# The end of a normalisation wave: one batch's output rows on VectorE, two batches normalised on ScalarE and GpSimd, low product parts issued last

## The reference, cut to what matters

```python
x = _layernorm(x + _L0_attn_ref(...))
x = _layernorm(x + _L0_ffn_ref(...))     # h = _layer_norm(h + interf, ln4_g[1], ln4_b[1]) is its last step
x = _layernorm(x + _L1_attn_ref(...))    # q, k = elu(x W) + 1; v = x W; kv = k^T v; z = 1 / (q . sum k); out = (q kv) z Wo
x = _layernorm(x + _L1_ffn_ref(...))     # six blocks of gelu(x W1 + b1) W2 + b2 + x
```

## Time and profile before

| what | value |
|---|---|
| median of 3 runs | 1039.43 us |
| lowest of them | 1037.92 us |
| the profiled execution's own time | 1038.4 us |
| its span, first to last instruction | 1036.7 us |
| mean granted TensorE clock over the span | 0.986 of full speed |
| TensorE busy | 986.6 us (95% of the span) |
| VectorE, ScalarE, GpSimd busy | 735.5, 606.8, 370.9 us |

### The profile page before, as it was taken

The page is one execution under the profiler, slowest core; times in us unless marked ns, Lnnn a source line. Parts: engine busy times, 40 slices in busy tenths (PEclk is TensorE's granted clock), DMA queues, the critical chain, the costliest instruction groups (busy, mean ns, idle before and its releaser), DMA issues.

```text
span 1036.7 us, 18193 instructions
## 1 busy us (share of the span) xinstructions
PE 986.6 (95%) x6627; PEld 824.5 (80%) x6627; DVE 735.5 (71%) x2003; ACT 606.8 (59%) x1177; POOL 370.9 (36%) x646
## 2 busy tenths in 40 slices
PE   6999999999999898889999999999999999999997
PEld 5555655555758797778899999999999999999997
DVE  5666787867647779867557768766776877677764
ACT  5566667655259774456546666554666655456660
POOL 4444374552131474443722222322222232222600
PEclk9899999998999999999999999999999999999999
DMA  7000000013020001022201010110101011010101
GB/s 254 23 2 21 3 22 22 23 43 102 22 87 4 1 2 41 1 102 62 82 1 42 1 41 1 42 41 2 41 1 42 1 41 42 1 42 1 41 23 60
DMA packets 29234, 36.91 MB, mean 36 GB/s; under 512 B 1780, under 2 KB 26584, under 8 KB 29144
## 3 DMA queue, kind: packets, MB, share of 16 engines
q1 hardware_dynamic: 24728, 31.15, 9.4%
q10 hardware_dynamic: 4416, 4.59, 1.4%
HBM read 31.40 MB, written 4.20 MB: 34 GB/s over the span
## 4 chain that ended last, share of the span: by engine, by line
PE 56%; DVE 4%; POOL 2%; issue 1%; ACT 1%; DVEq 0%; POOLq 0%; ACTq 0%
PE ps L1930 25%; PE ps L1947 24%; PE ps L1820 2%; PE ps L1902 2%; DVE ln_stats L2337 1%; PE ps L1960 1%; PE ps L1871 1%; POOL hs L1717 1%; POOL x_b L1717 0%; PE ps L1834 0%; DVE amp L2373 0%; PE ps L1849 0%; PE ps L1862 0%; PE ps L1771 0%; DVE att L2429 0%
## 5 line engine op out<-in xcount | busy, mean ns | idle before, releaser
L2173 ACT ACTIVATE G<-ps,bias_col 128x512 f32<-128x512 f32 x192 | 135.8, 707 | 176.5 <-PE ps L1930 167.9
L1947 PE MATMUL ps<-w_h,G_h 128*128 128x256 f32 x736 | 204.3, 278 | 0.0
L1947 PE MATMUL ps<-w_l,G_h 128*128 128x256 f32 x736 | 204.0, 277 | 0.0
L1947 PE MATMUL ps<-w_h,G_l 128*128 128x256 f32 x736 | 204.0, 277 | 0.0
L2477 DVE TENSOR_TENSOR G_l<-G,G_h 128x512 fp32r<-128x512 f32 x192 | 155.8, 819 | 59.7 <-ACT G_h L2174 59.7
L1747 POOL TENSOR_TENSOR x_a<-xn,mlp_g 128x1024 f32<-128x1024 f32 x20 | 68.0, 3401 | 333.8 <-DVE xn L2505 333.8
L708 ACT ACTIVATE probs<-ps 128x512 f32<-128x512 f32 (+3 forms) x256 | 98.3, 441 | 98.0 <-PE ps L848 97.2
L1930 PE MATMUL ps<-xT_h,w_h 128*128 128x512 f32 x384 | 151.7, 395 | 0.3 <-issue 0.3
L1930 PE MATMUL ps<-xT_h,w_l 128*128 128x512 f32 x384 | 149.9, 390 | 0.0
L1930 PE MATMUL ps<-xT_l,w_h 128*128 128x512 f32 x384 | 149.5, 389 | 0.0
L1119 DVE CUSTOM_DVE_ANT_0 ps<-ps,q_mask 128x128 f32<-128x128 f32 (+3 forms) x256 | 120.7, 512 | 29.9 <-PE ps L837 29.4
(11 more groups left out here) (320 smaller groups left out, 2094.5 us busy)
## 6 DMA issues: line engine op xcount, KB each, us to landing
w_raw<-L_ffn_W_T SPq DMA_DIRECT2D x12, 1024.0 KB, 5.1
hs<-L_attn_hidden_states SPq DMA_DIRECT2D x8, 512.0 KB, 3.9
x_kept<-hs SPq DMA_DIRECT2D x4, 512.0 KB, 3.2
w_raw<-x_kept SPq DMA_DIRECT2D x2, 1024.0 KB, 5.3
out<-xn SPq DMA_DIRECT2D x3, 512.0 KB, 3.0
w_raw<-L_ffn_ent_w_T SPq DMA_DIRECT2D x1, 1024.0 KB, 10.2
w_raw<-L_ffn_ent_pw SPq DMA_DIRECT2D x1, 1024.0 KB, 12.3
heads_T<-neg_rows SPq DMA_DIRECT2D x64, 2.0 KB
```

Source lines behind the costliest of these rows:

```text
L1947: mm = pe.matmul(ps[:, 4 + t // 2, (t % 2) * D:(t % 2 + 1) * D], x[b % 2][f][:, t * P:(t + 1) * P], w2_chunk(w, f), start=(k == 0), stop=( ...
L2173: act.activation(G32[n % 4], bank, ACT.Gelu, bias=bias)
```

## The change

Batch 0's output rows are made on VectorE (`output_rows`) and no longer on GpSimd. VectorE makes the low parts of batch 3's last turn ahead of `moments_sum(0)`, and `output_low(0)` ahead of `sum_up(1)`. For batches 2 and 3 `centre` and `sum_up` are gone: VectorE makes an offset (-mean x root, `offset_last`), ScalarE normalises from PSUM (`normalise_last`), GpSimd multiplies by the row last_g, and VectorE adds the residual (`add_residual`), later in its list than `sum_up` was; `moments_sum(2)` and `root("sum", 2)` are later in theirs too. The first unit of a batch waits for the high parts only, and issues its two products with low parts last; the first three units take the banks in the order 2, 0, 1.

```diff
-    ON_SCALAR = [key for b in range(B) for key in (("stage", END, b), ("sum", b))] + [("next", 0), ("next", 1)]
+    ON_SCALAR = [("stage", END, 0), ("sum", 0), ("stage", END, 1), ("sum", 1), ("stage", END, 2), ("stage", END, 3),
+                 ("sum", 2), ("sum", 3), ("next", 0), ("next", 1)]
...
+    def unit_bank(n):
+
+        return (n - 1) % 3 if n < 3 else n % 3
...
# GpSimd
-        for b in range(B):
+        whole(("sum", 1), g.x_b[:, RT:2 * RT, :], sums(1))
+        pool.wait_ge(rows_in, 16)
+        for b in (2, 3):
+            pool.wait_ge(wave["a_last"], b - 1)
+            pool.tensor_tensor(normed(b), normed(b), bcast(last_g, 1, [P, RT, D]), ALU.mult).then_inc(wave["g_gain"], 1)
+        for b in (2, 3):
             whole(("sum", b), g.x_b[:, b * RT:(b + 1) * RT, :], sums(b))
...
# TensorE, unit
             if at == 0:
-                pe.wait_ge(wave["v_tl"], wave_done(b))
-            if n == 2:
+                pe.wait_ge(wave["a_th"], wave_done(b))
+            if n == 0:
 
                 centred(pe, 1)
-            if n >= 3:
-                pe.wait_ge(second["a_exp"], n - 2)
-                pe.wait_ge(second["a_v"], values(n - 3))
...
+            if n >= RT - 1:
+                before = n - 2 if n < 5 else n - 3
+                pe.wait_ge(second["a_exp"], before + 1)
+                pe.wait_ge(second["a_v"], values(before))
...
+            if at == 0:
+                products = [products[k] for k in (0, 1, 3, 4, 2, 5)]
+            for i, (lhsT, rhs) in enumerate(products):
+                if at == 0 and i == 4:
+                    pe.wait_ge(wave["v_tl"], wave_done(b))
+                mm = pe.matmul(ps[:, unit_bank(n), :], lhsT, rhs, start=(i == 0), stop=(i == 5))
...
# ScalarE
+        def normalise_last(b):
+            root = rooted(act, "stage", END, b)[1]
+            act.wait_ge(wave["v_offset"], b - 1)
+            for k in range(RT):
+                ins = act.activation(normed(b)[:, k, :], banks(b)[k], ACT.Identity,
+                                     bias=offsets[:, b - 2, k:k + 1], scale=root[:, k:k + 1])
+            ins.then_inc(wave["a_last"], 1)
...
         unit(0, 2)
+        normalise_last(2)
         unit(0, 3)
+        root("stage", END, 3)
         unit(0, 4)
-        root("sum", 2)
         for c in range(KC):
             output_high(1, c)
         unit(0, 5)
+        normalise_last(3)
         unit(1, 0)
-        root("stage", END, 3)
         unit(1, 1)
         unit(1, 2)
+        root("sum", 2)
         unit(1, 3)
...
# VectorE
+        def offset_last(b):
+
+            moments, root = rooted(v, "stage", END, b)
+            v.scalar_tensor_tensor(offsets[:, b - 2, :], moments[:, :, 0], -1.0, root, ALU.mult, ALU.mult
+                                   ).then_inc(wave["v_offset"], 1)
+
+        def add_residual(b):
+
+            v.wait_ge(wave["g_gain"], b - 1)
+            chain.step(v.tensor_tensor(amp[:, b, :, :].rearrange("p c s -> p (c s)"),
+                                       normed(b).rearrange("p t d -> p (t d)"),
+                                       g.x_a[:, b * RT:(b + 1) * RT, :].rearrange("p t d -> p (t d)"), ALU.add))
+
+        def output_rows():
+
+            moments, root = rooted(v, "sum", 0)
+            for k in range(RT):
+                ins = v.tensor_scalar(g.x_b[:, k, :], sums(0)[:, k, :], moments[:, k, 0:1], root[:, k:k + 1],
+                                      ALU.subtract, ALU.mult)
+            ins.then_inc(wave["v_whole"], 1)
...
                 if (st, b) == (END - 1, B - 2):
                     centre(0)
                     sum_up(0)
+                elif (st, b) == (END - 1, B - 1):
                     run(moments_sum(0))
-                elif (st, b) == (END - 1, B - 1):
-                    run(moments(END, 1))
+                    steps = moments(END, 1)
+                    run(steps, 1)
+                    output_rows()
+                    run(steps)
...
         centre(1)
-        sum_up(1)
         for c in range(KC):
             output_low(0, c)
+        sum_up(1)
         run(moments_sum(1))
         unit(0, 0)
         run(moments(END, 2))
         unit(0, 1)
-        centre(2)
+        offset_last(2)
         unit(0, 2)
-        sum_up(2)
+        run(moments(END, 3))
         unit(0, 3)
-        run(moments_sum(2))
         unit(0, 4)
+        offset_last(3)
         for c in range(KC):
             output_low(1, c)
         unit(0, 5)
         block_diagonal(0)
-        run(moments(END, 3))
         unit(1, 0)
         divide(0, 0)
-        centre(3)
         unit(1, 1)
         divide(0, 1)
-        sum_up(3)
+        add_residual(2)
+        run(moments_sum(2))
         unit(1, 2)
         unit(1, 3)
         attention_low(0)
+        add_residual(3)
         run(moments_sum(3))
         unit(1, 4)
```

More of the change, by code:

```diff
@@ L246, in build @@
         g.wave = sems(top, nc, "a_trig v_turns v_h a_hh v_gated g_zero v_c p_lin v_mv g_scale g_chain a_norm p_T a_th v_tl a_l1 v_l1 v_chain "
-                      "v_scale v_mean a_root v_center g_eps", "wave_")
+                      "v_scale v_mean a_root v_center v_whole v_offset a_last g_gain g_eps", "wave_")
         g.second = sems(top, nc, "blocks_in b2_in g_ones p_unit a_exp a_v v_unit p_kv v_bd p_num v_att v_z p_attT a_atth v_attl "
@@ L1500, in rest @@
     eps = put(nc, "root_eps", g.small, ROOT + 14 * RT, [1])
+    offsets = put(nc, "root_offsets", g.small, ROOT + 16 * RT, [2, RT])
     TILE = NORM + 14 * RT
@@ L1542, in rest @@
     ON_VECTOR = [("stage", 0, 0)]
-    ON_SCALAR = [key for b in range(B) for key in (("stage", END, b), ("sum", b))] + [("next", 0), ("next", 1)]
-    WHOLE = [*(("sum", b) for b in range(B)), *(("next", b) for b in range(B))]
+    ON_SCALAR = [("stage", END, 0), ("sum", 0), ("stage", END, 1), ("sum", 1), ("stage", END, 2), ("stage", END, 3),
+                 ("sum", 2), ("sum", 3), ("next", 0), ("next", 1)]
+    WHOLE = [*(("sum", b) for b in range(1, B)), *(("next", b) for b in range(B))]
     ON_GPSIMD = [key for key in NORMS + WHOLE if key not in ON_VECTOR + ON_SCALAR]
@@ L1552, in normalised @@
     def normalised(eng, *key):
-        if key in WHOLE:
+        if key == ("sum", 0):
+            eng.wait_ge(wave["v_whole"], 1)
+        elif key in WHOLE:
             eng.wait_ge(second["g_whole"], WHOLE.index(key) + 1)
@@ L1559, in centred @@
     def centred(eng, b):
-        eng.wait_ge(wave["v_center"], b + 1)
+        if b < 2:
+            eng.wait_ge(wave["v_center"], b + 1)
+        else:
+            eng.wait_ge(wave["a_last"], b - 1)
     def rooted(eng, *key):
@@ L1801, in unit @@
             if at == 0:
-                pe.wait_ge(wave["v_tl"], wave_done(b))
-            if n == 2:
+                pe.wait_ge(wave["a_th"], wave_done(b))
+            if n == 0:
                 centred(pe, 1)
-            if n >= 3:
-                pe.wait_ge(second["a_exp"], n - 2)
-                pe.wait_ge(second["a_v"], values(n - 3))
-            i = 0
+            if n >= RT - 1:
+                before = n - 2 if n < 5 else n - 3
+                pe.wait_ge(second["a_exp"], before + 1)
+                pe.wait_ge(second["a_v"], values(before))
+            products = []
             for c in range(KC):
@@ L1818, in unit @@
                              (g.xT_l[:, b, c, cols], g.wkv_h[:, c, :]))
-                for lhsT, rhs in parts:
-                    mm = pe.matmul(ps[:, n % 3, :], lhsT, rhs, start=(i == 0), stop=(i == 5))
-                    i += 1
+                products += parts
+            if at == 0:
[4 more added lines that the diff above has]
+                mm = pe.matmul(ps[:, unit_bank(n), :], lhsT, rhs, start=(i == 0), stop=(i == 5))
             mm.then_inc(second["p_unit"], 1)
@@ L2106, in unit @@
                 act.wait_ge(second["v_unit"], n - 1)
-            act.activation(ex[:, n % 2, 0:width], ps[:, n % 3, 0:width], ACT.Exp)
-            act.activation(pos[:, n % 2, 0:width], ps[:, n % 3, 0:width], ACT.Relu).then_inc(second["a_exp"], 1)
+            act.activation(ex[:, n % 2, 0:width], ps[:, unit_bank(n), 0:width], ACT.Exp)
+            act.activation(pos[:, n % 2, 0:width], ps[:, unit_bank(n), 0:width], ACT.Relu).then_inc(second["a_exp"], 1)
             if j >= KC:
@@ L2114, in unit @@
                 act.activation(v1[:, b % 2, j - KC, :, 0:P],
-                               ps[:, n % 3, D:2 * D].rearrange("p (m n) -> p m n", m=KC),
+                               ps[:, unit_bank(n), D:2 * D].rearrange("p (m n) -> p m n", m=KC),
                                ACT.Copy).then_inc(second["a_v"], 1)
@@ L2338, in statistics @@
             chain.step(ins)
+            yield
             chain.settle()
```

## The result

The changed kernel takes 1043.48 us (median of 5 runs, 1043.2 to 1047.13) against 1039.1 us for the kernel before in the same comparison. The ratio is 1.0047, with a 95% interval of [1.0032, 1.0061]: about 4.4 us slower. One of the five runs of the kernel before took 2357.16 us; the ratio goes without it. The forecast was 1041.2 us with a range up to 1043.2, so the median lies 0.3 us outside. The profiled execution takes 1043.2 us, its span 1041.5 us, against 1038.4 and 1036.7.

What follows compares the result with a forecast made beforehand. TensorE, busy all its time from 497 us, was taken to bound the kernel by how late it gets there. A net delay of +1.8 us and +1.0 for the clock on 1038.4 gave 1041.2 us, range 1037.8 to 1043.2.

Steps and rivals of the forecast that it cites:

- The 9.0 us margin: Before the change, batch 2's rows lay ready at 423.93, 9.0 us before TensorE transposed them at 432.94.
- The lead ahead of it: Before final_turn(2, 0), TensorE was to run earlier: 1.8 us at final_turn(0), 0.3 at final_turn(1), 1.7 on reaching final_turn(2, 0).
- the walk had x_b end last: At final_turn(1): GpSimd's rows of batch 1 start at 410.6, take 5.75 us and end at 416.4, 0.3 us earlier.
- Rival (4): Before 423.7: ScalarE's eight added ACTIVATEs hold up its units, no lead arises, add_residual(2) is 1.7 us later; 1042.9 us, chance 0.08.
- Rival (3): TensorE's later waits at 440 to 470 us swallow the delay, clock holds: 1038.4 us, down to 1036.7; chance 0.14.
- Rival (1): Same stall at final_turn(2, 0) but no fall of TensorE's clock: +1.8, 1040.2 us, chance 0.2.
- Rival (2): GpSimd and VectorE exclude each other fully, x_b takes 6.1, clock stretch falls on work: +2.4 + 1.7, 1042.5 us, chance 0.08.
- GpSimd's multiply by last_g is done long before ... has 5 us to spare: Batch 2's multiply, ahead of add_residual(2), starts at 416.4, takes 4.03 us at worst and has 5 us to spare.
- that rule on x_b beside add_residual alone: At batch 2's rows: by the exclusion rule x_b would wait 1.21 us for the add, 6.1 instead of 5.5.
- the forecast had 11.70 us: From numerators(0, 1) at 423.7, through divide, residual, statistics, root and x_b (5.5 us), to final_turn(2, 0) at 435.4.
- The clock was taken at 1.0: Behind the 4.2 us stall TensorE's clock likely falls to half: loss between 0 and 1.7 us, taken as 1.0.
- has had time to finish: After the stall, the 0.67 us wait at 436.00 goes because ScalarE has finished root("sum", 3) before; 1.8 us remain.

Runs made afterwards that it cites:

- the two halves apart: Two kernels: the change with batches 2 and 3 as before, 1039.38 us; the kernel before with batches 2 and 3 alone changed, 1045.63 us.
- The run in pieces: The changed kernel with GpSimd's multiply by last_g cut into four instructions of 256 columns per batch: 1046.1 us, ratio 1.0045.
- the run with one input: The changed kernel with GpSimd's multiply by last_g replaced by a multiply by 1.0, last_g left out for batches 2 and 3: 1045.68 us, ratio 1.0051.
- the run with work in the stall: The changed kernel with 32 useless TensorE transposes of batch 1's rows added ahead of final_turn(2, 0): 1044.07 us, ratio 1.0035.
- the changed kernel's second profile: The changed kernel run once more without any edit, beside later runs on the same chip: 1045.7 us, ratio 1.0055.
- all three mended: The changed kernel with batch 2's rows on VectorE, GpSimd's multiply in four pieces, batch 3's residual, moments and root behind batch 2's parts: 1040.54 us, ratio 1.0001.
- The first half: The changed kernel with batches 2 and 3 as in the kernel before: 1039.38 us, ratio 0.999.

## Why the prediction was right in kind and short in size

*Right.* Direction, place and mechanism: a stall at final_turn(2, 0), released by GpSimd's x_b, because batch 2's sum now hangs on divide(0, 1). The 9.0 us margin that the prediction pointed at was spent, and the two halves apart show the whole loss there. The lead ahead of it came as walked, to 0.1 us at three marks of TensorE. At two of them part of that is luck. At final_turn(1) the walk had x_b end last; x_b took 5.18 us for the 5.75, lay ready 0.54 us before, and TensorE's own list, with its 1.53 and 0.44 us for ScalarE, ended last there. At unit (1, 0) TensorE came without a wait; the walk had the high parts end last. Rival (4) falls with these marks. Rival (3) falls with the spacing from project(0) on, 57.15 against 57.07 us: nothing later absorbs a delay. Rival (1) falls with the windows: the clock did fall. Rival (2) gave 1042.5 with x_b held for 6.1 us and 1.7 for the clock; x_b took 5.89, and in both terms the rival was nearer than the forecast. It has the hold of the multiply as little as the forecast.

*What failed: the step "GpSimd's multiply by last_g is done long before ... has 5 us to spare".* It asked only whether batch 2's multiply is done in time, which it is (417.66), not what a multiply does to VectorE while it runs (a term put at nothing without a reason), and it did not place batch 3's at all. Batch 2's held the q step in front of batch 1's low parts and block_diagonal(0); batch 3's, from 420.49 to 422.87, held VectorE's two-input k step, which took 2.14 us. The lead at numerators(0, 1) was gone, 1.65 us later than forecast. The run in pieces and the run with one input give 1.0 and 1.33 us of it back; the cause of the last 0.3 is open. The Trainium skill (SBUF — State Buffer, Who interferes with whom) says that a VectorE instruction with two SBUF inputs contends with a GpSimd instruction that reads SBUF (the on-chip memory that holds all these operands); the prediction weighed that rule on x_b beside add_residual alone, and not on the multiply that the change adds. For the two-input multiply the trace agrees (1.54 and 2.14 us, each ended just behind GpSimd); beside one-input GpSimd instructions, which read SBUF too, it shows no such hold: VectorE went on in 0.69 and 0.82 us, the second 0.4 longer than alone.

*Two terms were mis-sized.* From numerators(0, 1) to final_turn(2, 0) the forecast had 11.70 us and 12.37 were measured: 0.39 is x_b (5.89 for 5.5), the rest hand-overs. The clock was taken at 1.0; the run with work in the stall measures 1.6, next to its upper bound of 1.7; in the changed kernel's second profile, with 6.8 us at half, the same stretch took 5.07 us. From final_turn(2, 0) to project(0) that is 4.27 us against 3.77 (40.95 - 37.51 - 0.67 + 1.0). Together 1.65 + 0.67 + 0.50 = 2.8 us on the forecast +2.8: the 5.6 measured at project(0). That the spans differ by 4.8 only is the early start of 0.87 us, which is scatter. Two sums in the working are slightly off, and nothing hangs on them: 406.4 + 1.8 + 1.41 + 0.38 is 409.99 and not 409.95, and with x_b at 4.87 the delay would be 1.2 and not 1.4.

*Not seen at all, and hidden by the stall:* batch 3's residual, moments and root, which the change puts ahead of batch 2's high and low parts. The prediction said of ScalarE's root("sum", 3) only that it "has had time to finish". It costs nothing while GpSimd is later; alone, with batch 2's rows on VectorE, it cost 4.11 us of waiting.

*Open:* how often a run gets a longer half-speed stretch. The five runs of the kernel after have mean clocks of 0.988 (1043.2 us) to 0.983 (1047.13), so part of any difference of 1 to 2 us between these kernels may be that. In three profiles (in pieces, work in the stall, all three mended) the clock also fell between 464 and 470, where no wait above 1.33 us lies near; the other ten, with the same waits, show no fall there. Why is open. The first half, which has no new stall, is the only part with a gain, and needs root("sum", 2) moved to show it.

## What to carry to other kernels

When a step moves to another engine, look beside it as well as behind it: for each new instruction, list which instructions of the other engines lie in its time and read the same memory, not only whether its result is in time. When a step's margin is spent on purpose, walk every list that now holds it, because the wait that ends last hides the next one in line: here taking the 4.7 us away uncovered 4.1, and moving three steps together gave the time back (whether two of them would do was not run). A stall of TensorE costs more than its length when the clock falls behind it; useless work in the stall shows how much, 1.6 us here up to project(0).

## What the runs showed of the hardware

VectorE's two-input step of 0.42 us lasted 2.14 beside one GpSimd two-input multiply over 1024 columns, 0.43 beside the same multiply in four pieces (but another step then took 1.27 for 0.68), and 0.82 beside a one-input GpSimd instruction, which itself took 2.77 to 3.01 us where the two-input multiply took 2.38 and 2.60. TensorE's granted clock was at half (1.2 of 2.4 GHz) from 436.9 to 440.3 us behind the 4.71 us stall in one profile of the changed kernel and from 437.0 to 443.8 in the other; with transposes in the stall and 1.24 us of waiting it was at full speed there. In all seven profiles with a TensorE wait of 3.00 to 4.73 us between 400 and 460 us the clock fell in or just behind that wait; in the six whose waits there are at most 1.73 us it held until 460.
